# Scatters in pairs behind named matmul groups, and fills behind the second score pass

## The chip, the cores and the metric

The kernel runs on one core of one Trainium2 chip. The metric is the time of one execution on the device, in microseconds, as the median of several runs. Engines are named as the profile names them: PE (TensorE), DVE (VectorE), ACT (ScalarE), POOL (GpSimd) and SP (SyncE).

## The reference

For `x` of 16 x 512 tokens with 256 features in float32:

```
xn  = layernorm(x)
att = softmax(causal(rope(xn Wq) rope(xn Wk)^T / 4)) (xn Wv) Wo      # 16 heads of 16
s   = softmax(xn router_w^T + router_bias);  top 4 of 32 experts, their scores rescaled to a sum of 1
moe = sum over the 4 of score * down_e(silu(gate_e xn) * up_e xn)    # hidden size 128
sh  = (silu(xn sgate^T) * (xn sup^T)) sdown^T                        # shared, hidden size 512
out = x + att + moe + sh
```

## The kernel before, in words

`block_kernel` runs three phases. Phase A (`phase_a`) goes over the 16 batches of 512 tokens and computes layernorm, attention, the shared network and the routing. It also writes each token's normalised row, once for each of its four experts, into that expert's region of the DRAM tensor `values`, and a small entry (where the result goes, and its weight) into `table`. Phase B/C (`phase_bc`) is the expert loop: 288 blocks of 128 rows are loaded from `values`, go through their expert, and are scattered to `y_dram`. Phase D adds the four results of each token and the rest, and stores `out`.

**Order of the work in phase A.** All engines walk one list of steps, `ORDER`, from line 74. Each engine has a table of handlers (`run`, and the dictionaries that are given to it) and carries out, in the list's order, the steps that it has a handler for. Nothing reorders an engine's own queue: an instruction that waits for a semaphore holds up all behind it on that engine. Steps named in `NEXT_STEPS` (layernorm, xT, qk, vr, part0, part1, partsT, stack, route and the ranks) work on the next batch, so the list overlaps batch b's attention with batch b+1's projections. The first and second batch's steps are written out, batches 1 to 14 are a hardware loop, and the last batch (`last_steps`) leaves the next-batch steps out.

**The steps that matter here.**
- `s1 g u` (PE, L949 and L952) makes the scores of heads of group g in their first form; DVE (L745) takes their row maxima. `negsplit` (DVE) splits the negative maxima into three bf16 parts, `negT` transposes them (PE L962, ACT L595), and SP (L403) copies them by DMA into extra rows of `q_st`. `s2 g u` (PE L982 and L993) then makes the transposed scores with the maxima already subtracted; it waits for that DMA at u = 0. ACT (L607) takes the exponential of each s2 group.
- s1 and s2 write to two PSUM units in turn (`ps_u`), so a group waits for the reader of the group but one before it: DVE's maximum for an s1, ACT's exponential for an s2.
- `qk t` for tile t of the next batch: PE projects (L911), DVE applies the rotary factors (L706, L709) into two buffers, POOL adds them into `rqk` (L472), ACT copies that to bf16 in step `part0` (L542), POOL subtracts (L474), ACT copies the rest in step `part1` (L547), POOL subtracts again (L476). PE transposes the three parts in `partsT` (L923). All of POOL's part is one handler, at the step `qk t`; ACT's parts stand at their own places in the list, among exponentials.
- `copy` (ACT L585) copies the normalised rows to `xs` once all scatters of the batch before have landed (`scattered`); DVE's `rankC` waits for the same and makes `slot`.
- `scat t` (POOL L487, L489) issues, for the four choices of tile t, one indirect DMA to `table` and one to `values`: 8 for a step, 32 for a batch. Steps scat 0 and 1 stand early in the list, after `gth 1` and `gth 2`; scat 2 and 3 stand after `partsT 3` and `s2 3 0`, behind qk 3.
- `fill` (POOL L495), in the last batch alone, behind scat 3: 32 indirect DMAs of zero rows, one for each expert, so that the last block of each region is complete. Phase A ends when `filled` and `scattered` have their full counts and SP's last store has landed.

What the scatter step and its neighbours on POOL's queue look like before:

```
def scatter(b, step, env):
    t = step[1]
    pool.wait_ge(xs_ready, NT * b + NT)
    pool.wait_ge(slots, b + 1)
    hold(pool, passed_pool)
    for k in range(TOPK * t, TOPK * (t + 1)):
        ...
run(pool, {"loaded": loaded, "qk": qkv, "scat": scatter, "fill": fill})
```

Of the kernel before, what the change touches and what calls it, by code (L numbers as in the profile page):

```python
# [34 lines left out]
BATCH, SEQ, D = 16, 512, 256  # L35
NT = SEQ // P
KC = D // P
NH, DH = 16, 16
NG, GH = 4, 4
E, TOPK, HE, HS = 32, 4, 128, 512  # L40
NM = HS // P
# [19 lines left out]
NU1 = len(MAX_UNITS)  # L61
NU2 = GH + 1


def hold(eng, passed):


    eng.sem_inc(passed, 1)
# [4 lines left out]

ORDER = [
    ("rankC",), ("gate", 0), ("placeV",), ("s1", 0, 0), ("gth", 0), ("up", 0), ("s1", 0, 1), ("copy",), ("s1", 0, 2),
    ("gate", 1), ("s1", 0, 3), ("s1", 0, 4), ("gth", 1), ("scat", 0), ("up", 1), ("lnA",), ("gate", 2), ("s1", 0, 5),
    ("negsplit", 0), ("gth", 2), ("scat", 1), ("s1", 1, 0), ("up", 2), ("s1", 1, 1), ("negT", 0), ("gate", 3),
# [11 lines left out]
    ("exps",), ("stack", 1), ("down", 0), ("down", 1), ("rankA",), ("av", 3, 0), ("av", 3, 1), ("av", 3, 2),  # L89
    ("av", 3, 3), ("rankB",), ("down", 2), ("avT", 3), ("down", 3), ("aT", 0), ("aT", 1), ("oproj", 0), ("oproj", 1),  # L90
]


def attention_steps(with_next):
# [3 lines left out]
def last_steps(order):  # L98


    s, piece = [], 0
    for step in order:
        s.append(step)
        if step == ("rankC",):
            s.append(("fill_rows",))
        if step == ("scat", NT - 1):
            s.append(("fill",))
        if step[0] == "s2" and step[1:] != (0, 0) and piece < GU_PIECES:
            s.append(("load_gu", piece))
            piece += 1  # L110
        if step == ("s2", NG - 1, NU2 - 1):
            s += [("load_d", k) for k in range(D_PIECES)]
    assert piece == GU_PIECES
    return s
# [75 lines left out]
def phase_a(nc, sb_, sem, ident, identb, iota_e, counts, we_gu, we_d, ps_g, ps_u, ps_av, x, wqkvr, wgu_e, wd_e, wo, wgu_s, wd_s, bias,  # L190
            rope_cos, rope_sin, values, sum_dram, table):
    stack = ExitStack()
    with stack:
        def sb(name, shape, dt=F32):
            return sb_(name, shape, dt, stack)

        def carve(space):
# [3 lines left out]
            def take(shape, dt=F32):  # L201
# [6 lines left out]
                if len(names) == 1:  # L208
# [54 lines left out]
        av = sb("av", [P, SEQ])  # L263
# [5 lines left out]
        gth = sb("gth", [P, SEQ])  # L269
# [18 lines left out]
        slot = sb("slot", [P, NT * TOPK], I32)  # L288
        dest_f = sb("dest_f", [P, NT * TOPK])
        entry = sb("entry", [P, NT * TOPK, 2], I32)  # L290
        xs = sb("xs", [P, NT, D])
# [4 lines left out]
        xs_ready, slots = sem("xs_ready"), sem("slots")  # L296
# [3 lines left out]
        scattered = sem("scattered")  # L300
# [4 lines left out]
        we_in, fill_chain, fill_ready, filled = sem("we_in"), sem("fill_chain"), sem("fill_ready"), sem("filled")  # L305
        neg_parts, tanh_done, av_out, exps, chosen_ready = \
            sem("neg_parts"), sem("tanh_done"), sem("av_out"), sem("exps"), sem("chosen_ready")
        pe = {n: sem("pe_" + n) for n in ("xT", "qk", "vr", "qT", "kT", "gate", "up", "s1", "negT", "s2", "av", "avT",
                                          "aT", "sum", "rank")}
# [11 lines left out]
        block = stack.enter_context(nc.Block())  # L321
        body = attention_steps(True)
        tail = last_steps(attention_steps(False))


# [96 lines left out]
        def _(pool):  # L422
# [56 lines left out]
                    chain.closed()  # L479

            def scatter(b, step, env):
                t = step[1]
                pool.wait_ge(xs_ready, NT * b + NT)
                pool.wait_ge(slots, b + 1)
                hold(pool, passed_pool)
                for k in range(TOPK * t, TOPK * (t + 1)):
                    pool.indirect_dma_start(table[:, :], bass.IndirectOffsetOnAxis(ap=slot[:, k:k + 1], axis=0),  # L487
                                            entry[:, k, :], None).then_inc(scattered, 16)
                    pool.indirect_dma_start(values[:, :], bass.IndirectOffsetOnAxis(ap=slot[:, k:k + 1], axis=0),  # L489
                                            xs[:, k // TOPK, :], None).then_inc(scattered, 16)  # L490

            def fill(b, step, env):
                pool.wait_ge(fill_ready, 1)
                for e in range(E):
                    pool.indirect_dma_start(values[:, :], bass.IndirectOffsetOnAxis(ap=fill_row[:, e:e + 1], axis=0),  # L495
                                            zeros[:, :], None, bounds_check=E * REGION - 1, oob_is_err=False
                                            ).then_inc(filled, 16)

            def loaded(b, step, env):
                if step[1] == 1:  # L500
# [6 lines left out]
                    pool.wait_ge(table_set, 16)  # L507

            run(pool, {"loaded": loaded, "qk": qkv, "scat": scatter, "fill": fill})
            pool.wait_ge(filled, 16 * E)  # L510
            pool.wait_ge(scattered, SCATTERS * BATCH)
# [983 lines left out]
```

## Time and profile before

| | before |
|---|---|
| median of 3 runs | 2137.58 us (2136.33 to 2138.6) |
| profiled execution, its span | 2641.3 us (no other time is given for this execution) |
| PE busy | 1935.0 us, 73% |
| POOL busy | 1063.8 us, 40% |
| DVE busy | 1290.2 us, 49% |
| ACT busy | 929.5 us, 35% |
| mean granted clock of PE | 0.847 |

The runs are executions without the profiler; the profiled one is longer by 503.7 us. Phase A takes the first 1945 us of the profiled span, the expert loop the stretch to about 2525, phase D the rest. A row of a timeline gives the start in us from the span's start, the busy time in us, engine, line and operation, and in brackets how long the engine was idle before it and what ended that wait.

### The profile page before, as it was taken

What the parts mean: (1) busy time and instruction counts of PE and PEld (TensorE: products, weight loads), DVE (VectorE), ACT (ScalarE), POOL (GpSimd) and SP (SyncE); (2) the same over time, 40 slices, a digit from 0 to 9 for tenths busy, and PEclk for the clock granted to TensorE, in tenths of its full rate; (3) what the DMA queues carried; (4) which work ended last, traced back from release to release, by engine and by line L of the source; (5) the groups of instructions that cost most, each with busy time, mean ns of one, the idle gap of its engine ahead of it and who ended that gap; (6) DMA issues with size and microseconds to landing.
All of it is one profiled execution on the core that took longest, in us unless ns stands there. A gap on an engine that the chain in (4) does not pass through costs nothing. (4 is left out here: it accounts for less than half of the span.)

```text
span 2641.3 us, 43971 instructions
## 1 busy us (share of the span) xinstructions
PE 1935.0 (73%) x11495; PEld 1234.2 (47%) x11496; DVE 1290.2 (49%) x3379; ACT 929.5 (35%) x1953; POOL 1063.8 (40%) x1056
## 2 busy tenths in 40 slices
PE   5677778787767878777887877874479898998900
PEld 2344444444434444444544444442257777777700
DVE  4445345364534536453453535442235555555567
ACT  2324252443415244242534424341224444444400
POOL 5444343343434334443433444246215544554500
PEclk8888788898878888887988888887689999999955
DMA  5150423415052341505225051432455554545389
GB/s 107 63 97 21 93 40 64 64 40 96 19 94 40 64 64 40 96 22 90 47 57 88 17 100 30 78 59 76 132 158 159 153 150 146 155 144 152 112 304 331
DMA packets 242512, 255.07 MB, mean 97 GB/s; under 512 B 74357, under 2 KB 216190, under 8 KB 242304
## 3 DMA queue, kind: packets, MB, share of 16 engines
q1 hardware_dynamic: 184768, 161.63, 28.4%
q0 software_dynamic: 35840, 71.63, 8.6%
q10 hardware_dynamic: 21824, 20.98, 2.5%
q14 instruction: 60, 0.49, 0.1%
q8 instruction: 20, 0.33, 0.1%
HBM read 112.54 MB, written 94.64 MB: 78 GB/s over the span
## 5 line engine op out<-in xcount | busy, mean ns | idle before, releaser
L745 DVE TENSOR_REDUCE neg<-ps_u 128x2 f32<-128x768 f32 (+3 forms) x384 | 392.4, 1043 | 380.7 <-PE ps_u L952 237.2
L487 POOL DMA_INDIRECT table<-entry,slot x256 | 248.0, 969 | 536.2 <-ACT xs L585 435.4
L982 PE MATMUL ps_u<-we_d 99*128 99x512 bf16 (+3 forms) x1024 | 246.1, 353 | 250.1 <-DMA we_d<-neg_t 121.6
L607 ACT ACTIVATE probs<-ps_u 128x1024 f32<-128x1024 f32 x320 | 323.1, 1027 | 286.6 <-PE ps_u L993 189.2
L1244 POOL DMA_INDIRECT y_dram<-yb,ent x288 | 283.0, 983 | 278.8 <-issue 164.9
L489 POOL DMA_INDIRECT values<-xs,slot x256 | 252.3, 986 | 83.4 <-issue 83.4
L933 PE MATMUL ps_g<-we_gu 128*128 128x512 f32 x512 | 257.7, 634 | 38.1 <-DVE hid L728 32.1
L949 PE MATMUL ps_u<-we_d 96*128 96x128 bf16 (+3 forms) x1024 | 232.2, 312 | 72.4 <-ACT probs L607 26.6
L982 PEld LDWEIGHTS ps_u<-we_d 99*128 99x128 bf16 x1024 | 96.5, 107 | 397.5 <-issue 221.4
L911 PE MATMUL ps_g<-we_gu 128*128 128x512 f32 (+1 forms) x512 | 199.7, 514 | 2.4 <-ACT we_gu L564 2.4
L472 POOL TENSOR_TENSOR rqk<-we_gu 128x512 f32<-128x512 f32 x64 | 81.3, 1270 | 266.2 <-DVE we_gu L709 263.3
L767 DVE RECIPROCAL rden<-ps_g 128x16 f32<-128x16 f32 x64 | 16.3, 255 | 348.8 <-issue 250.2
L1281 PE MATMUL ps_av<-we_gu,x_t 128*128 x576 | 157.9, 399 | 36.5 <-DVE x_t L1369 34.5
L1012 PE MATMUL ps_av<-probs,v_pad 128*32 128x512 f32 (+3 forms) x2048 | 165.9, 447 | 23.8 <-issue 22.6
L949 PEld LDWEIGHTS ps_u<-we_d 96*128 96x128 bf16 x1024 | 94.1, 100 | 190.5 <-issue 59.8
L1295 PE MATMUL ps_u<-we_d,h_t 128*128 x576 | 177.6, 391 | 0.0
L952 PE MATMUL ps_u<-mask_qk,identb 128*128 128x128 bf16 (+2 forms) x704 | 177.2, 252 | 0.0
L993 PE MATMUL ps_u<-mask_kq,identb 128*128 128x256 bf16 (+1 forms) x640 | 132.6, 291 | 52.1 <-issue 52.1
L933 PEld LDWEIGHTS ps_g<-we_gu 128*128 128x128 f32 x512 | 97.2, 200 | 132.1 <-issue 80.5
L1281 PE MATMUL ps_g<-we_gu,x_t 128*128 x576 | 155.4, 394 | 4.1 <-issue 4.1
L1369 DVE COPY x_t<-ps_g 128x256 f32<-128x256 f32 x288 | 120.6, 419 | 67.9 <-issue 44.8
L616 ACT ACTIVATE av<-ps_av 128x512 f32<-128x512 f32 x64 | 37.8, 591 | 299.6 <-remote 212.1
(158 smaller groups left out, 3247.4 us busy)
## 6 DMA issues: line engine op xcount, KB each, us to landing
we_d<-we_gu SPq DMA_DIRECT2D x384, 128.0 KB, 5.9
xg<-values SPq DMA_DIRECT2D x288, 128.0 KB
ys<-y_dram SPq DMA_DIRECT2D x64, 512.0 KB, 5.4
we_gu<-x SPq DMA_DIRECT2D x16, 512.0 KB
xres<-x SPq DMA_DIRECT2D x16, 512.0 KB
sum_dram<-osum SPq DMA_DIRECT2D x16, 512.0 KB, 3.2
we_gu<-wgu_e ACTq DMA_DIRECT2D x16, 512.0 KB
sums_in<-sum_dram SPq DMA_DIRECT2D x8, 1024.0 KB
```

The lines of the kernel that those rows point to most:

```text
L487: pool.indirect_dma_start(table[:, :], bass.IndirectOffsetOnAxis(ap=slot[:, k:k + 1], axis=0), entry[:, k, :], None).then_inc(scattered, 16)
L489: pool.indirect_dma_start(values[:, :], bass.IndirectOffsetOnAxis(ap=slot[:, k:k + 1], axis=0), xs[:, k // TOPK, :], None).then_inc(scatte ...
L607: nc.scalar.activation(probs[g % 2][:, u, :], ps_u[env[1][step][0]][:, :, :].rearrange("p a n -> p (a n)"), ACT.Exp, scale=SCALE).then_inc ...
L745: nc.vector.tensor_reduce(neg[:, g % 2, i, h0:h0 + nh], src, AX.X, ALU.max, negate=True).then_inc(S["row_max"], 1)
L911: ins = nc.tensor.matmul(ps[:, 0:n], xn_t[:, c, t * P:(t + 1) * P], w_qkvr[:, c, lo:lo + n], start=(c == 0), stop=(c == KC - 1))
L933: ins = nc.tensor.matmul(ps[:, :], w_gu[:, c, lo:lo + P], xn_t[:, c, :], start=(c == 0), stop=(c == KC - 1))
L949: nc.tensor.matmul(ps[:, a, k * n:(k + 1) * n], q_st[0:KROWS, h, i * P:(i + 1) * P], k_st[0:KROWS, h, 0:n], start=(k == 0), stop=False, sk ...
L952: ins = nc.tensor.matmul(dst, identb[:], mask_qk[:].rearrange("p (o n) -> p o n", o=1).broadcast_to([P, per_bank, P]), start=False, stop=T ...
L982: nc.tensor.matmul(ps[:, a, lo:lo + n], k_st[0:MROWS, h, kt * P:(kt + 1) * P], q_st[0:MROWS, h, kt * P:SEQ], start=(lo == 0), stop=False, ...
L1244: pool.indirect_dma_start(y_dram[:, :], bass.IndirectOffsetOnAxis(ap=ent[k][:, 0:1], axis=0), yb[k][:, :], None, bounds_check=TOKENS * TOP ...
L1281: ins = nc.tensor.matmul(ps_gu[s][:, 0:2 * HE], x_t[s][:, c * P:(c + 1) * P], w_gu[:, bass.ds(e, 1), c, :], start=(c == 0), stop=(c == KC ...
L1295: nc.tensor.matmul(ps_y[s][:, 0:D], h_t[s][:], w_d[:, bass.ds(e, 1), :], start=True, stop=True).then_inc(y_ps, 1)
```

## The change

`scat` becomes 16 steps instead of 4. Step k issues one pair: the DMA to `table` and the DMA to `values` of column k of `slot`. Each waits first for a matmul group that `SCAT_AFTER[k]` names, by PE's semaphore for it; only k = 0 waits for `xs_ready` and `slots`. In `ORDER` the 16 steps are spread over the list, each behind its group. Nothing else in the list changes place. The 32 fills of the last batch become 16 steps of two, each behind an s2 group that `FILL_AFTER` names. The number of DMAs is the same.

```
--- before.py
+++ after.py
 ORDER = [
     ("rankC",), ("gate", 0), ("placeV",), ("s1", 0, 0), ("gth", 0), ("up", 0), ("s1", 0, 1), ("copy",), ("s1", 0, 2),
-    ("gate", 1), ("s1", 0, 3), ("s1", 0, 4), ("gth", 1), ("scat", 0), ("up", 1), ("lnA",), ("gate", 2), ("s1", 0, 5),
...
+    ("gate", 1), ("s1", 0, 3), ("scat", 0), ("s1", 0, 4), ("gth", 1), ("up", 1), ("scat", 1), ("lnA",), ("gate", 2),
+    ("s1", 0, 5), ("scat", 2), ("negsplit", 0), ("gth", 2), ("s1", 1, 0), ("up", 2), ("scat", 3), ("s1", 1, 1),
+    ("negT", 0), ("gate", 3), ("lnB",), ("lnC",), ("gth", 3), ("up", 3), ("scat", 4), ("s2", 0, 0), ("s2", 0, 1),
+    ("s2", 0, 2), ("s1", 1, 2), ("scat", 5), ("xT", 0), ("xT", 1), ("xT", 2), ("s1", 1, 3), ("s1", 1, 4), ("qk", 0),
+    ("s2", 0, 3), ("vr", 0), ("xT", 3), ("vr", 1), ("part0", 0), ("s1", 1, 5), ("negsplit", 1), ("s2", 0, 4),
+    ("scat", 6), ("qk", 1), ("part1", 0), ("negT", 1), ("s1", 2, 0), ("s1", 2, 1), ("part0", 1), ("av", 0, 0),
+    ("av", 0, 1), ("s1", 2, 2), ("s2", 1, 0), ("scat", 7), ("av", 0, 2), ("av", 0, 3), ("s1", 2, 3), ("partsT", 0),
+    ("s1", 2, 4), ("s1", 2, 5), ("scat", 8), ("part1", 1), ("avT", 0), ("qk", 2), ("s2", 1, 1), ("s2", 1, 2),
+    ("negsplit", 2), ("partsT", 1), ("s2", 1, 3), ("scat", 9), ("part0", 2), ("qk", 3), ("s2", 1, 4), ("negT", 2),
+    ("part1", 2), ("vr", 2), ("s1", 3, 0), ("s1", 3, 1), ("scat", 10), ("part0", 3), ("av", 1, 0), ("av", 1, 1),
...
+    ("av", 2, 2), ("av", 2, 3), ("s2", 3, 0), ("scat", 14), ("s2", 3, 1), ("avT", 2), ("stack", 0), ("s2", 3, 2),
+    ("s2", 3, 3), ("scat", 15), ("rank",), ("s2", 3, 4),
...
+SCAT_AFTER = [("s1", 0, 3), ("up", 1), ("s1", 0, 5), ("up", 2), ("up", 3), ("s1", 1, 2), ("s2", 0, 4), ("s2", 1, 0),
+              ("s1", 2, 5), ("s2", 1, 3), ("s1", 3, 1), ("s2", 2, 0), ("s2", 2, 3), ("s2", 2, 4), ("s2", 3, 0),
+              ("s2", 3, 3)]
+
+
+FILL_AFTER = [(0, 3), (0, 4), (1, 0), (1, 1), (1, 2), (1, 3), (1, 4), (2, 0), (2, 1), (2, 2), (2, 3), (2, 4), (3, 0),
+              (3, 1), (3, 2), (3, 3)]
+FILLS = 2
...
-        if step == ("scat", NT - 1):
-            s.append(("fill",))
+        if step[0] == "s2" and step[1:] in FILL_AFTER:
+            s.append(("fill", FILL_AFTER.index(step[1:])))
...
             def scatter(b, step, env):
-                t = step[1]
-                pool.wait_ge(xs_ready, NT * b + NT)
-                pool.wait_ge(slots, b + 1)
+                k = step[1]
+                after = SCAT_AFTER[k]
+                if after[0] == "s1":
+                    pool.wait_ge(pe["s1"], NG * NU1 * b + NU1 * after[1] + after[2] + 1)
+                elif after[0] == "s2":
+                    pool.wait_ge(pe["s2"], NG * NU2 * b + NU2 * after[1] + after[2] + 1)
+                else:
+                    pool.wait_ge(pe["up"], NM * b + after[1] + 1)
+                if k == 0:
+                    pool.wait_ge(xs_ready, NT * b + NT)
+                    pool.wait_ge(slots, b + 1)
                 hold(pool, passed_pool)
-                for k in range(TOPK * t, TOPK * (t + 1)):
...
+                pool.indirect_dma_start(table[:, :], bass.IndirectOffsetOnAxis(ap=slot[:, k:k + 1], axis=0),
+                                        entry[:, k, :], None).then_inc(scattered, 16)
+                pool.indirect_dma_start(values[:, :], bass.IndirectOffsetOnAxis(ap=slot[:, k:k + 1], axis=0),
+                                        xs[:, k // TOPK, :], None).then_inc(scattered, 16)
 
             def fill(b, step, env):
-                pool.wait_ge(fill_ready, 1)
-                for e in range(E):
+                k = step[1]
+                if k == 0:
+                    pool.wait_ge(fill_ready, 1)
+                pool.wait_ge(pe["s2"], NG * NU2 * (BATCH - 1) + NU2 * FILL_AFTER[k][0] + FILL_AFTER[k][1] + 1)
+                for e in range(FILLS * k, FILLS * (k + 1)):
```

## Rows read from the trace of the kernel before

**Rows 1.** The page: its span, and one of its costliest groups.

```profile
span 2641.3 us, 43971 instructions
...
L1244 POOL DMA_INDIRECT y_dram<-yb,ent x288 | 283.0, 983 | 278.8 <-issue 164.9
```

**Rows 2.** Windows of one batch: start:end, length, each engine's busy time, clock, DMA share, GB/s.

```profile
994.00:1004.00 10.00, 9.97 (x42) 4.68 (x41) 9.41 (x20) 1.19 (x2) 7.05 (x8) 1.00 0.31 104
...
1020.50:1024.00 3.50, 3.48 (x15) 1.75 (x15) 1.61 (x4) 1.94 (x2) 0.00 (x0) 0.50 0.00 0
...
1044.00:1054.00 10.00, 10.00 (x90) 5.89 (x89) 6.43 (x12) 7.03 (x11) 4.71 (x5) 1.00 0.00 1
...
1070.00:1083.40 13.40, 2.57 (x7) 0.62 (x6) 0.00 (x0) 0.00 (x0) 7.74 (x8) 0.50 0.99 163
1083.40:1089.00 5.60, 5.53 (x31) 3.60 (x31) 0.68 (x2) 4.47 (x5) 0.00 (x0) 0.50 0.00 0
...
sum 115.70, PE 88.80 PEld 50.88 DVE 56.02 ACT 42.72 POOL 45.64; mean PE 6.34 PEld 3.63 DVE 4.00 ACT 3.05 POOL 3.26
```

**Rows 3.** Timeline of POOL, one batch: start, us, line, op, idle before and releaser.

```profile
1030.30 1.27 POOL L472 TENSOR_TENSOR rqk<-we_gu 128x512 f32<-128x512 f32 x1 [15.43 <-DVE we_gu L709]
...
1035.90 1.27 POOL L472 TENSOR_TENSOR rqk<-we_gu 128x512 f32<-128x512 f32 x1 [0.24 <-DVE we_gu L709]
...
1042.92 1.15 POOL L476 TENSOR_TENSOR we_gu<-we_gu 128x512 bf16<-128x512 f32 x1 [3.85 <-ACT we_gu L547]
1045.88 1.27 POOL L472 TENSOR_TENSOR rqk<-we_gu 128x512 f32<-128x512 f32 x1 [1.80 <-DVE we_gu L709]
...
1052.96 1.27 POOL L472 TENSOR_TENSOR rqk<-we_gu 128x512 f32<-128x512 f32 x1 [0.17 <-POOL we_gu L476]
...
1058.36 1.16 POOL L476 TENSOR_TENSOR we_gu<-we_gu 128x512 bf16<-128x512 f32 x1 [2.23 <-ACT we_gu L547]
1059.67 0.99 POOL L487 DMA_INDIRECT table<-entry,slot  x1 [0.15 <-issue]
1060.96 0.97 POOL L489 DMA_INDIRECT values<-xs,slot  x1 [0.31 <-issue]
...
1109.74 0.97 POOL L487 DMA_INDIRECT table<-entry,slot  x1 [29.68 <-ACT xs L585]
...
1225.43 0.97 POOL L487 DMA_INDIRECT table<-entry,slot  x1 [29.93 <-ACT xs L585]
```

**Rows 4.** Timeline of ACT in the same batch.

```profile
1037.21 0.63 ACT L542 ACTIVATE we_gu<-rqk 128x512 bf16<-128x512 f32 x1 [1.70 <-POOL rqk L472]
...
1048.92 0.66 ACT L542 ACTIVATE we_gu<-rqk 128x512 bf16<-128x512 f32 x1
...
1054.27 0.63 ACT L542 ACTIVATE we_gu<-rqk 128x512 bf16<-128x512 f32 x1 [2.42 <-POOL rqk L472]
```

**Rows 5.** Timeline of PE in the same batch.

```profile
1040.74 0.38 PE L949 MATMUL ps_u<-we_d 96*128 96x512 bf16 x1
...
1050.82 0.38 PE L949 MATMUL ps_u<-we_d 96*128 96x256 bf16 x2
...
1056.35 0.39 PE L949 MATMUL ps_u<-we_d 96*128 96x512 bf16 x1
...
1086.41 1.06 PE L982 MATMUL ps_u<-we_d 99*128 99x512 bf16 x3
```

**Rows 6.** Window from the last batch's first scatter to its last matmul.

```profile
1792.00:1941.00 149.00, 71.27 (x441) 38.51 (x439) 34.69 (x57) 27.36 (x33) 62.51 (x64) 0.71 0.39 129
```

**Rows 7.** Timelines of POOL, SP and PE, last batch: its ends, the negative-row transfer.

```profile
1792.57 0.97 POOL L487 DMA_INDIRECT table<-entry,slot  x1 [29.38 <-ACT xs L585]
...
1873.30 0.98 POOL L495 DMA_INDIRECT values<-zeros,fill_row  x1 [0.30 <-issue]
...
1813.80 104.16 SPq L403 DMA_DIRECT2D we_d<-neg_t  x4
...
1816.14 1.01 PE L982 MATMUL ps_u<-we_d 99*128 99x512 bf16 x3 [9.41 <-DMA we_d<-neg_t]
```

More of the change, by code:

```diff
@@ L75 @@
     ("rankC",), ("gate", 0), ("placeV",), ("s1", 0, 0), ("gth", 0), ("up", 0), ("s1", 0, 1), ("copy",), ("s1", 0, 2),
-    ("gate", 1), ("s1", 0, 3), ("s1", 0, 4), ("gth", 1), ("scat", 0), ("up", 1), ("lnA",), ("gate", 2), ("s1", 0, 5),
-    ("negsplit", 0), ("gth", 2), ("scat", 1), ("s1", 1, 0), ("up", 2), ("s1", 1, 1), ("negT", 0), ("gate", 3),
[11 rows of a table removed]
+    ("gate", 1), ("s1", 0, 3), ("scat", 0), ("s1", 0, 4), ("gth", 1), ("up", 1), ("scat", 1), ("lnA",), ("gate", 2),
+    ("s1", 0, 5), ("scat", 2), ("negsplit", 0), ("gth", 2), ("s1", 1, 0), ("up", 2), ("scat", 3), ("s1", 1, 1),
+    ("negT", 0), ("gate", 3), ("lnB",), ("lnC",), ("gth", 3), ("up", 3), ("scat", 4), ("s2", 0, 0), ("s2", 0, 1),
[9 rows of a table added]
+    ("negsplit", 3), ("route",), ("partsT", 3), ("s2", 2, 4), ("scat", 13), ("negT", 3), ("av", 2, 0), ("av", 2, 1),
+    ("av", 2, 2), ("av", 2, 3), ("s2", 3, 0), ("scat", 14), ("s2", 3, 1), ("avT", 2), ("stack", 0), ("s2", 3, 2),
+    ("s2", 3, 3), ("scat", 15), ("rank",), ("s2", 3, 4),
     ("exps",), ("stack", 1), ("down", 0), ("down", 1), ("rankA",), ("av", 3, 0), ("av", 3, 1), ("av", 3, 2),
@@ L481, in scatter @@
             def scatter(b, step, env):
-                t = step[1]
-                pool.wait_ge(xs_ready, NT * b + NT)
-                pool.wait_ge(slots, b + 1)
-                hold(pool, passed_pool)
-                for k in range(TOPK * t, TOPK * (t + 1)):
[L487 to L490, printed above, removed]
-            def fill(b, step, env):
-                pool.wait_ge(fill_ready, 1)
-                for e in range(E):
+                k = step[1]
[9 more added lines that the diff above has]
+                    pool.wait_ge(slots, b + 1)
+                hold(pool, passed_pool)
+                pool.indirect_dma_start(table[:, :], bass.IndirectOffsetOnAxis(ap=slot[:, k:k + 1], axis=0),
+                                        entry[:, k, :], None).then_inc(scattered, 16)
+                pool.indirect_dma_start(values[:, :], bass.IndirectOffsetOnAxis(ap=slot[:, k:k + 1], axis=0),
+                                        xs[:, k // TOPK, :], None).then_inc(scattered, 16)
+            def fill(b, step, env):
+                k = step[1]
[3 more added lines that the diff above has]
+                for e in range(FILLS * k, FILLS * (k + 1)):
                     pool.indirect_dma_start(values[:, :], bass.IndirectOffsetOnAxis(ap=fill_row[:, e:e + 1], axis=0),
```

13 rows, old and new, of the table ORDER are left out of this document.

## The prediction

> **What bounds the kernel now.** The page comes first [rows 1]: the profiled span is 2641.3 us and the median of the runs 2137.58 us, 503.7 us less. So part of what the trace shows cannot be in the runs, and the first question is which part. The windows of one batch [rows 2] show it: while POOL issues long bursts of scatters, all other engines stand nearly still (from 1070.0 to 1083.4 PE is busy 2.57 of 13.4 us, DVE and ACT not at all), and after such a stretch TensorE's granted clock is 0.50, the 1.2 GHz level, for a few us. Between bursts (1044 to 1054) PE is busy 10.0 of 10 us at clock 1.00: there the order of PE's work is the bound.
>
> **Budget.** A batch lasts 115.7 us (1109.74 to 1225.43 [rows 3]), PE is busy 88.80 of it [rows 2], idle 26.9. There are 15 such batches: 403.5 us. The last batch has 149.0 − 71.3 = 77.7 us of idle [rows 6]. The two windows at clock 0.50 (3.5 and 5.6 us) would take half at the full clock: 4.55 a batch, some 73 us in all. Together 554 us could vanish, and 504 have. What is left, 50 us or 3.1 us a batch, is about what plain waits between PE, ACT and DVE need. I read it so: the standstills belong to the profiled execution, and in the runs a batch takes about 86 us with PE nearly always busy. The other bound: the expert loop's scatters (L1244 [rows 1]) are idle 278.8 us, 164.9 of it their own pace; if the other 114 us were missing from the runs as well, (50 + 114) / 16 = 10.3 us of idle a batch would still be real, 7 above the plain waits.
>
> **The change, part by part.**
>
> *Removed: bursts of 16 scatters.* Each batch issues the same 32 scatters, so POOL's total is the same. What a burst could cost in the runs is a late transfer of the negative row maxima, which s2 waits for. In the last batch that transfer is issued at 1813.80, amid 64 indirect DMAs without a gap from 1792.57 on, and s2 starts at 1816.14 [rows 7]: 2.3 us. That is short, so I take a gain of 0; the bounds are 0 and 7 us a batch (above).
>
> *Moved: four pairs into the middle of the rope chain.* On POOL's queue pair 6 now stands ahead of qk 1, pairs 7 and 8 ahead of qk 2, pair 9 ahead of qk 3. Before, nothing stood there. Two scatters are 1.29 us apart start to start and the first begins 0.15 us after a tensor operation ends (1059.67, 1060.96 [rows 3]), so a pair takes 2.6 us and two take 5.1. All four matmul groups that they name are done by the time POOL arrives, so the gates wait for nothing. I follow the chain POOL, ACT, PE, since part0 stands on ACT's queue ahead of an exponential, and that exponential frees the PSUM unit that PE's next group but one needs:
> - qk 0 ends at 1035.66 (0.24 before 1035.90 [rows 3]); pair 6 runs to 1038.3; rqk 1 starts at 1038.5, not 1035.90: +2.6. part0 of tile 1 moves from 1037.21 [rows 4] to 1039.8, the exponential of s2(1,0) behind it ends at 1041.4, and s1(2,4) starts at 1041.5, not 1040.74 [rows 5]: PE +0.8. The last subtraction of qk 1 waited 3.85 us for ACT [rows 3], so it loses only 1.0: it ends at 1045.1, not 1044.07.
> - pairs 7 and 8 run to 1050.2; rqk 2 starts at 1050.4, not 1045.88 [rows 3]: +4.5. part0 of tile 2 goes from 1048.92 [rows 4] to 1051.7, s2(1,4)'s exponential ends at 1053.3, s1(3,1) starts at 1053.4, not 1050.82 [rows 5]: PE +2.6 by now. qk 2 ends at 1055.7, not 1052.79: +2.9.
> - pair 9 runs to 1058.3; rqk 3 starts at 1058.5, not 1052.96: +5.5. part0 of tile 3 already waited for it (2.42 us [rows 4]), so it moves from 1054.27 to 1059.8, s2(2,0)'s exponential ends at 1061.8, and s1(3,4) starts at 1061.9, not 1056.35 [rows 5]: PE +5.6 by now.
>
> With a little for the register arithmetic of four gates: 5.7 us a batch. PE has no idle time afterwards in which to win it back (88.8 us busy [rows 2], 84 of it at the full clock, in a batch of 86 to 91). The 15 batches that work on a next one pay it: 85.5 us. Bounds: 2.6 a batch if ACT and PE absorb the last step, 7.5 if each pair costs 3.0 us and a wait more.
>
> *Moved: the other pairs.* Pairs 0 to 5 take 15.6 us between the copy and rope 0, where POOL waited 15.43 us beside its burst (1030.30 [rows 3]), some 4 without the standstill; pair 5, gated by s1(1,2), is over before that rope. Pairs 10 to 15 go out behind qk 3, the last behind s2(3,3) (from 1086.41 [rows 5] to 1087.3), over by 1090, with the copy just before 1109.74. Cost 0, hidden by POOL's wait before the copy (29.68 us [rows 3], some 13 of it left without the standstills); were it gone, each further us would be on ACT's copy.
>
> *The last batch.* It has no rope work. Before, POOL issued 64 indirect DMAs solidly from 1792.57 to 1874.3 [rows 7]. PE ended at 1941.0, but less 77.7 of idle, with some 5 for the clock and 5 of plain waits given back to either side, at about 1864: in the runs POOL ends this phase, by some 8 us. After, POOL is idle in part until s2(0,3), about 1812.5 without the wait of 9.41 us [rows 7]; from there 26 pairs (16 of fills, 10 of scatters) at 2.58 keep it busy for 67 us, to 1879.6: +5. Bounds 0 and 10.
>
> Sum: 85.5 + 5 = 90.5 us more; on the median of the runs, 2228 us. Against the profiled execution itself the sum would be 2732, but the profile of the changed kernel will not show that: spread pairs should not bring the standstills, so its span should fall, to some 2300 to 2500 us, while the runs get longer.
>
> **A rule that would make it worse.** In the window 994 to 1004, DVE is busy 9.41 of 10 us and POOL's scatters keep their 0.97 us, as they do at 1070 to 1083.4 with DVE idle (7.74 us for 8) [rows 2]: DVE doesn't hold them up. The Trainium skill, SBUF — State Buffer, section on the two separate sides, says that GpSimd cannot write descriptors for its DMAs while a VectorE operation in a two-port mode holds their shared port. The windows with both busy speak against it for these operations. By that rule the time would be nearer to the 2348 us of the last but one rival.
>
> **The rivals.**
> - *Faster.* The standstills are partly real, at the start of s2(0,0) and of s2(3,0), up to 7 us a batch, and single pairs end them: 16 × 7 = 112 less. With half of the chain's cost (2.6 × 15 + 5 = 44) the time is 2070; with a gain of 6 a batch, 2086. It decides from the point where the real stall exceeds what the pairs cost the rope chain. For it: the 163 GB/s and DMA share 0.99 at 1070 [rows 2]. Against: the budget, and the 2.3 us of the transfer. Taken as 2085. Chance 0.13.
> - *A smaller loss.* The chain delays PE only up to s1(3,1), +2.6 a batch, or the gain takes half of it: 39 + 5, 2182. Chance 0.15.
> - *No change.* POOL frees itself for the next tensor operation as soon as a DMA is handed on, so a pair costs nothing, or gain and loss cancel: 2138. Chance 0.04. Against: 0.97 us busy for each.
> - *DVE holds up the pairs in the rope chain* by one reduce of about 1 us for each of 8 scatters: 8 more a batch, 2137.6 + 15 × 13.7 + 5 = 2348. Chance 0.02.
> - *The gates do nothing*, each being open already when POOL comes to it: for pairs 6 to 9 this is so and is part of the forecast; for all 16 it would leave the same cost in the rope chain.
>
> **How the numbers follow.** The forecast, 2228, has 0.66 and a range of its own from 2195 to 2258: the cost of a batch from 4 to 7.5, with 0 to 10 for the end. With the smaller loss, from 2150 up, this holds about 0.8. 0.2% (4 us) is about what a measurement of this kernel can tell. Slower by more: 0.66 + 0.15 + 0.02 = 0.83; within it 0.04; faster 0.13.
>
> **What would show it.** In the profile after: POOL's rqk of tiles 1 to 3 start right after a scatter and not on DVE; ACT's part0 waits for POOL by several us each; PE waits for ACT's exponential at s1(3,1) and s1(3,4); the idle of 29.7 us before the copy shrinks; 64 indirect DMAs end the phase. It is wrong if these waits are there and the time is not above 2142 (then the standstills were real in part), or if rqk 2 and 3 start no later, against their ropes, than before.

## The result and the profile after

The changed kernel takes 2208.51 us (median of 4 runs, 2199.36 to 2209.38); the kernel before, beside it, 2136.95 us. The ratio is 1.033, with a 95% interval of 1.0309 to 1.035: 71.6 us slower. Forecast were 90.5 us more (2228 us, range 2150 to 2258).

One plain fact has to be known before the traces are compared. The kernel before does not take the same time on every chip: in the series below it took 2137 us on one chip and 2639 to 2642 us on three others, and in all series the profiled execution was as long as the runs beside it. The trace of before that stands above has a span of 2641.3 us and a mean granted clock of 0.847, where the runs of before in the series have 0.94 on the one chip and 0.85 on the three, so I take it to be of the second sort; the runs of before that stand beside it are of the first, and so are the runs and the trace (span 2197.5) of the changed kernel that are shown here. I call them chips without and with standstills, for short: each chip was used in one series alone, so that it is the chip, and not something that changed from series to series, is not shown. Rows of the two traces can be compared in the stretches without a standstill only.

The page of the changed kernel, span, busy time and the costliest group on POOL (to be held against [rows 1]):

```profile
span 2197.5 us, 44375 instructions
...
PE 1819.5 (83%) x11495; PEld 1188.7 (54%) x11496; DVE 1276.1 (58%) x3379; ACT 923.8 (42%) x1953; POOL 1064.8 (48%) x1056
...
L506 POOL DMA_INDIRECT table<-entry,slot x256 | 249.7, 975 | 441.3 <-PE ps_u L974 322.1
```

One batch of it in a window (the sum row of [rows 2] is the one before). A batch lasts 89.0 us here (791.62 to 880.64 on POOL) and 89.9 in the mean of 14, from POOL's rqk of tile 0 to the next batch's. PE is busy 80.75 us of the window and the clock is 0.98 of the full one, so no standstill is in it:

```profile
880.00:969.00 89.00, 80.75 (x550) 48.10 (x548) 53.09 (x126) 42.12 (x67) 45.84 (x44) 0.98 0.39 69
```

POOL in that batch, start and busy time first, idle time and releaser in brackets ([rows 3] before). The rqk of tile 0 starts at 900.48, before at 1030.30; so 129.82 us are added to compare. Tile 1 then starts at 1038.11 (before 1035.90, +2.2), tile 2 at 1049.65 (1045.88, +3.8), tile 3 at 1057.23 (1052.96, +4.3), each with no idle time behind a scatter. From tile 0 to tile 3 it is 26.93 us in the median of 15 batches, and 22.66 before. The rows:

```profile
900.48 1.26 POOL L484 TENSOR_TENSOR rqk<-we_gu 128x512 f32<-128x512 f32 x1 [2.12 <-DVE we_gu L731]
...
908.29 1.28 POOL L484 TENSOR_TENSOR rqk<-we_gu 128x512 f32<-128x512 f32 x1
...
913.69 1.15 POOL L488 TENSOR_TENSOR we_gu<-we_gu 128x512 bf16<-128x512 f32 x1 [2.23 <-ACT we_gu L569]
...
919.83 1.28 POOL L484 TENSOR_TENSOR rqk<-we_gu 128x512 f32<-128x512 f32 x1
...
927.41 1.27 POOL L484 TENSOR_TENSOR rqk<-we_gu 128x512 f32<-128x512 f32 x1
...
934.12 0.98 POOL L506 DMA_INDIRECT table<-entry,slot  x1
...
948.87 0.97 POOL L508 DMA_INDIRECT values<-xs,slot  x1 [0.30 <-issue]
```

ACT's part0 of tiles 1 to 3 ([rows 4] before) waits for POOL, 4.70 us at the last, where it was 2.42:

```profile
909.60 0.63 ACT L564 ACTIVATE we_gu<-rqk 128x512 bf16<-128x512 f32 x1 [3.90 <-POOL rqk L484]
...
921.13 0.63 ACT L564 ACTIVATE we_gu<-rqk 128x512 bf16<-128x512 f32 x1 [1.60 <-POOL rqk L484]
...
928.72 0.63 ACT L564 ACTIVATE we_gu<-rqk 128x512 bf16<-128x512 f32 x1 [4.70 <-POOL rqk L484]
```

PE at the three places of the forecast, and the next batch's last wait for the negative rows ([rows 5] before). Shifted by 129.82, s1(2,4) is 0.3 us late, s1(3,1) 1.7 and s1(3,4) 4.3, and the two longer waits are put down to ACT's exponential:

```profile
911.19 0.39 PE L971 MATMUL ps_u<-we_d 96*128 96x512 bf16 x1
...
922.73 0.39 PE L971 MATMUL ps_u<-we_d 96*128 96x256 bf16 x2 [1.30 <-ACT probs L629]
...
930.80 0.39 PE L971 MATMUL ps_u<-we_d 96*128 96x512 bf16 x1 [2.67 <-ACT probs L629]
...
943.21 0.59 PE L1004 MATMUL ps_u<-we_d 99*128 99x512 bf16 x3 [0.83 <-DMA we_d<-neg_t]
```

The end of the last batch ([rows 7] before): POOL, then PE's last group, then two windows. POOL issues its last DMA at 1505.67, 5 us after PE is done, and the next phase begins 9.55 us after that one is over. The DMA engines are idle for most of this wait, with a share of 0.08 up to 1511 and 0.00 behind it:

```profile
1505.67 0.97 POOL L508 DMA_INDIRECT values<-xs,slot  x1 [0.30 <-issue]
1516.19 0.37 POOL L1254 IOTA blk_i<- 32x288 f32 x1 [9.55 <-POOLq L205]
```

```profile
1496.81 3.72 PE L1073 MATMUL ps_u<-w_o,attn_t 128*128 128x256 f32 x16 [0.25 <-ACT attn_t L644]
```

```profile
1506.00:1511.00 5.00, 0.00 (x0) 0.00 (x0) 0.00 (x0) 0.00 (x0) 0.64 (x1) 0.50 0.08 26
1511.00:1516.00 5.00, 0.00 (x0) 0.00 (x0) 0.00 (x0) 0.00 (x0) 0.00 (x0) 0.50 0.00 0
```

Over the whole run PE waits 64.7 us for the exponential ahead of an s1 group; with the four pairs out of the chain (e1, below) it is 2.3 us:

```profile
PE ps_u L971 <- ACT probs L629: 64.7, 34, 5.3
```

```profile
PE ps_u L971 <- ACT probs L629: 2.3, 7, 0.7
```

The difference, 62.4 us, is as much as this execution (2199.36 us, the fastest of the four) takes beyond the 2136.95 of before. The other three take 2208 to 2209 us, with a mean granted clock of 0.931 to 0.933 where this one has 0.939 and the runs of before on the first series' chip 0.940 to 0.944. So the 9 us between them are not in this trace, and a lower clock goes with them.

### The profile page after: what moved, and what is told of

Its sections match the earlier page's. It is cut to its first block and busy times, and to the rows that moved or that the text cites. A ratio compares the mean times of both kernels' runs of the same rounds, so it can differ in the third digit from the quotient of the medians.

```text
span 2197.5 us, 44375 instructions
## 1 busy us (share of the span) xinstructions
PE 1819.5 (83%) x11495; PEld 1188.7 (54%) x11496; DVE 1276.1 (58%) x3379; ACT 923.8 (42%) x1953; POOL 1064.8 (48%) x1056
## 5 line engine op out<-in xcount | busy, mean ns | idle before, releaser
L629 ACT ACTIVATE probs<-ps_u 128x1024 f32<-128x1024 f32 x320 | 317.8, 1023 | 140.2 <-PE ps_u L1015 138.8
L971 PE MATMUL ps_u<-we_d 96*128 96x128 bf16 (+3 forms) x1024 | 225.2, 304 | 95.3 <-ACT probs L629 64.7
L955 PE MATMUL ps_g<-we_gu 128*128 128x512 f32 x512 | 242.8, 607 | 3.0 <-DVE gth L742 2.9
L1004 PE MATMUL ps_u<-we_d 99*128 99x512 bf16 (+3 forms) x1024 | 199.0, 307 | 29.1 <-ACT probs L629 9.0
L1004 PEld LDWEIGHTS ps_u<-we_d 99*128 99x128 bf16 x1024 | 88.7, 99 | 129.4 <-issue 57.2
L1034 PE MATMUL ps_av<-probs,v_pad 128*32 128x512 f32 (+3 forms) x2048 | 156.0, 440 | 0.6 <-ACT probs L629 0.6
L1398 DVE TENSOR_SCALAR wh<-ent 128x1 f32<-128x1 f32 x288 | 44.3, 154 | 173.4 <-ACT tnh L1213 137.1
L599 ACT ACTIVATE we_gu<-ps_g 128x512 f32<-128x512 f32 x64 | 38.2, 597 | 219.1 <-PE ps_g L955 219.1
L1303 PEld LDWEIGHTS ps_av<-we_gu,x_t 128*128 128x128 f32 x576 | 102.0, 198 | 43.1 <-issue 34.8
L1227 ACT ACTIVATE yb<-ps_u 128x256 f32<-128x256 f32 x288 | 110.3, 383 | 34.1 <-PE ps_u L1317 8.3
```

Source lines behind the costliest of these rows:

```text
L629: nc.scalar.activation(probs[g % 2][:, u, :], ps_u[env[1][step][0]][:, :, :].rearrange("p a n -> p (a n)"), ACT.Exp, scale=SCALE).then_inc ...
L955: ins = nc.tensor.matmul(ps[:, :], w_gu[:, c, lo:lo + P], xn_t[:, c, :], start=(c == 0), stop=(c == KC - 1))
L971: nc.tensor.matmul(ps[:, a, k * n:(k + 1) * n], q_st[0:KROWS, h, i * P:(i + 1) * P], k_st[0:KROWS, h, 0:n], start=(k == 0), stop=False, sk ...
L1004: nc.tensor.matmul(ps[:, a, lo:lo + n], k_st[0:MROWS, h, kt * P:(kt + 1) * P], q_st[0:MROWS, h, kt * P:SEQ], start=(lo == 0), stop=False, ...
L1303: ins = nc.tensor.matmul(ps_gu[s][:, 0:2 * HE], x_t[s][:, c * P:(c + 1) * P], w_gu[:, bass.ds(e, 1), c, :], start=(c == 0), stop=(c == KC ...
```

## The experiments

Twelve runs in four series. The first (e1, e6, e7, e8) ran on a chip without standstills (before 2136.69 us, 9 runs), the second (e2, e3, e4, e5), third (e9, e10, e11) and fourth (e12) on three chips with them (2639.25, 2641.85 and 2640.54 us). Times are compared within a series.

### First series: which pairs cost what

**e1_chain_free.** Pairs 6 to 9 go behind qk 3, all else as changed.

```
-    ... ("s2", 0, 4), ("scat", 6), ("qk", 1), ... ("s2", 1, 0), ("scat", 7), ... ("s1", 2, 5), ("scat", 8), ...
-    ... ("s2", 1, 3), ("scat", 9), ("part0", 2), ("qk", 3), ...
+    ... ("s2", 1, 3), ("part0", 2), ("qk", 3), ("scat", 6), ("scat", 7), ("scat", 8), ("scat", 9), ...
```

> The changed kernel with pairs 6 to 9 moved behind qk 3 on POOL's queue, gates and fills unchanged. Theory A (the loss is POOL's pairs in the rope chain, some 4.3 us a batch by the trace after, and the rest is the end of the last batch): 2144 us, 2138 to 2150, 65 below the changed kernel. Theory B (the gates, or the spreading itself, cost time wherever the pairs stand): it stays near 2208. Theory C (bursts also hold PE up in the runs, and single pairs gain that back): with the chain free the gain shows, below 2130.

Measured: 2227.9 us (2222.28 to 2233.4), ratio 1.042 [1.0392, 1.0447]. All three theories missed. POOL and DVE show why; POOL first, rqk of tile 3 and the last scatter of the batch, then DVE's `rankC`, then PE:

```profile
844.87 1.27 POOL L484 TENSOR_TENSOR rqk<-we_gu 128x512 f32<-128x512 f32 x1 [0.17 <-POOL we_gu L488]
...
876.09 0.97 POOL L508 DMA_INDIRECT values<-xs,slot  x1 [0.30 <-issue]
```

```profile
885.02 0.18 DVE L860 TENSOR_TENSOR entry<-pr,zs 128x16 f32<-128x16 f32 x1 [5.48 <-DMA values<-xs,slot]
```

```profile
888.13 0.50 PE L971 MATMUL ps_u<-we_d 96*128 96x384 bf16 x1 [4.78 <-DVE neg L767]
```

The chain is free: rqk of tile 3 follows tile 2 after 0.17 us, as before. But ten pairs now stand behind qk 3; the last is issued at 876.09, over at 877.06, and `rankC`, which waits for `scattered`, starts at 885.02: the last scatter lands 8 us after POOL is done with it. DVE stands idle 5.48 us, and PE 4.78 us behind it. Over the whole run this wait is 74.5 us in 15 batches; PE's wait for DVE's maxima ahead of an s1 group grows by 65.5 us (14.0 in the changed kernel, 79.5 here), and its wait for the exponential falls by 62.4 (64.7 to 2.3). So the loss of the chain was given back at another place, and the cover that I had counted on for the pairs behind qk 3 is thin.

That alone does not make the kernel slower than the changed one. PE is also busy for longer, 1841.2 us against 1819.5, with the same instructions: behind the wait of 4.78 us its granted clock is 0.50, the 1.2 GHz level, for some 5 us of its work (888 to 893).

```profile
888.00:890.00 2.00, 1.87 (x6) 1.02 (x7) 1.87 (x4) 0.00 (x0) 0.00 (x0) 0.50 0.00 0
890.00:892.00 2.00, 2.00 (x4) 0.74 (x3) 1.48 (x2) 0.00 (x0) 0.00 (x0) 0.50 0.00 0
```

The three together, −62.4 + 65.5 + 21.7, give 24.8 us more than the changed kernel; the two profiled executions differ by 30.9.

The same run settles what a burst does on such a chip. Windows of the stretch with scatters and SP's stack copies (cf. 1070 to 1083.4 in [rows 2]: DMA share 0.99, 163 GB/s, PE busy 2.57 of 13.4):

```profile
861.00:871.00 10.00, 9.72 (x78) 6.57 (x79) 2.32 (x10) 4.64 (x7) 7.56 (x8) 1.00 1.14 169
871.00:881.00 10.00, 9.75 (x50) 7.65 (x49) 2.07 (x4) 1.52 (x3) 4.84 (x5) 1.00 1.12 180
```

DMA share and GB/s are higher than there, the row of scatters is longer (20), and PE is busy 9.72 and 9.75 of 10 us.

**e6_pair9_only** and **e7_pair6_only.** Of the four pairs one stays in the chain, the others go behind qk 3.

```
e6:  ... ("s2", 1, 3), ("scat", 9), ("part0", 2), ("qk", 3), ("scat", 6), ("scat", 7), ("scat", 8), ...
e7:  ... ("s2", 0, 4), ("scat", 6), ("qk", 1), ... ("qk", 3), ("scat", 7), ("scat", 8), ("scat", 9), ...
```

> Pair 9 alone stays ahead of qk 3; 6, 7 and 8 go behind it. Theory A: rqk of tile 3 followed qk 2 at once before the change and ACT waited for it, so one pair there costs its full 2.2 us a batch: 15 x 2.2 = 33 above the kernel with a free chain, 2177 us. If the loss were shared evenly by the four pairs it would be 16, 2160. Theory B: near 2208.

> Pair 6 alone stays ahead of qk 1; 7, 8 and 9 go behind qk 3. Theory A: the chain has slack there (POOL's last subtraction of tile 1 waited 3.85 us for ACT before), PE loses 0.3 us a batch: 2144 + 4 = 2148. Shared evenly: 2160. Theory B: near 2208.

Measured: 2216.64 us (2215.53 to 2221.15) and 2193.39 us (2187.94 to 2195.68). Both are some 40 us above the expectation of theory A, and the wait of `rankC` that e1 showed is nearly as long. The waits, in us in total, times, longest, first e6, then e7:

```profile
DVE entry L860 <- DMA values<-xs,slot: 40.3, 15, 5.0
...
PE ps_u L971 <- ACT probs L629: 37.7, 19, 2.4
```

```profile
DVE entry L860 <- DMA values<-xs,slot: 43.2, 15, 5.1
...
PE ps_u L971 <- ACT probs L629: 2.3, 7, 0.7
```

With nine pairs behind qk 3 the wait of `rankC` is 40.3 and 43.2 us, 2.7 to 2.9 a batch, against 5.0 with ten and none with six. Taking it off leaves 2176.3 and 2150.2 us, where 2177 and 2148 were expected for the chain. So close an agreement is in part luck: the same taken off e1 leaves 2153.4, 9 above the 2144 expected, and PE itself waits for DVE only 32.8 and 35.2 us longer than in the changed kernel (46.8 and 49.2 against 14.0), which would leave 2183.8 and 2158.2. The difference of the two kernels, 23.3 us or 1.6 a batch, does not depend on it: pair 9 costs more than pair 6, and they do not share evenly. PE's wait for the exponential says the same, 37.7 us with pair 9 alone and 2.3 with pair 6 alone, as in e1.

**e8_six_pairs.** Pairs 10 and 11 too stand ahead of qk 3, with gates that are open.

```
-    ... ("s2", 1, 3), ("scat", 9), ("part0", 2), ("qk", 3), ...
+    ... ("s2", 1, 3), ("scat", 9), ("part0", 2), ("scat", 10), ("scat", 11), ("qk", 3), ...
```

> Pairs 10 and 11 too stand ahead of qk 3, six pairs in the chain in place of four (their gates name s2(1,3)). Theory A: no slack is left there, so the two cost their full 2 x 2.5 us a batch: 15 x 5.1 = 77 above the changed kernel, 2285 us. Theory B: no difference, 2208.

Measured: 2296.95 us (2294.46 to 2299.17), 88 above the changed kernel, 77 expected. PE's wait for the exponential ahead of an s1 group, in the changed kernel and here:

```profile
PE ps_u L971 <- ACT probs L629: 64.7, 34, 5.3
```

```profile
PE ps_u L971 <- ACT probs L629: 140.3, 34, 10.4
```

It grows by 75.6 us, 5.0 a batch, which is what two pairs take on POOL (2 x 2.55). The chain has no slack left, as expected. The profile shows where the other 12 us can lie: PE is busy 1843.0 us, 23.5 longer than in the changed kernel with the same instructions, at a mean granted clock of 0.911 against 0.939.

### Second and third series: gates, fills, bursts

**e2_no_gates.** The handler without its waits for matmul groups; the order on POOL's queue is the same.

```
 def scatter(b, step, env):
     k = step[1]
-    after = SCAT_AFTER[k]
-    if after[0] == "s1":
-        pool.wait_ge(pe["s1"], ...)
...
     if k == 0:
```

> The changed kernel without the waits for matmul groups; the order on POOL's queue is the same. Pairs 0 to 5 then go out in one stretch behind the copy and 10 to 15 behind qk 3. Theory A: the four pairs in the rope chain stay where they are and their gates were open anyway, so the batches keep their loss and only the last batch starts earlier: 2204, 2198 to 2210. Theory B (the waits themselves cost): falls by 20 or more, under 2190. If the gates had saved something by thinning the DMAs, it rises above 2212.

Measured: 2517.95 us (2512.79 to 2522.68), before 2639.25, ratio 0.954. The numbers expected were for the other sort of chip, and whether closed gates cost or save anything there is not tested. Twelve scatters in a row behind the copy, and twelve behind qk 3, go with waits of PE that are longer than the changed kernel's on such a chip (4.28 and 3.08 us at the same places, e11 below); the first is at the end of the batch before, the longest of its kind, the second at s2(0,0):

```profile
802.43 4.49 PE L1027 MATMUL ps_av<-probs,v_pad 128*32 128x512 f32 x32 [11.30 <-ACT probs L622]
...
854.02 1.04 PE L997 MATMUL ps_u<-we_d 99*128 99x512 bf16 x3 [6.56 <-ACT probs L622]
```

**e3_fills_paired.** The kernel before, with the fills alone in gated pairs; the fill handler and `FILL_AFTER` as in the change.

```
-        if step == ("scat", NT - 1):
-            s.append(("fill",))
+        if step[0] == "s2" and step[1:] in FILL_AFTER:
+            s.append(("fill", FILL_AFTER.index(step[1:])))
```

> The kernel before, with the fills alone in 16 pairs behind the second score pass. Theory A: POOL is busy without a gap from the copy on in either order, so the last batch ends at the same time: 2137, 2133 to 2141. Rival: the gated fills themselves make the end later, 2142 to 2150. All other batches have their bursts: if the standstills belong to the profiled execution, the profile here shows a span several hundred us above its runs.

Measured: 2606.48 us (2604.58 to 2607.36), ratio 0.9875 [0.9858, 0.9892]; span of the profiled execution 2603.9. The last sentence of the expectation is refuted: the execution is as long as its runs. So the standstills are in all runs on these chips. The pairing of the fills saves 33 us here; what it does on a chip without standstills this run cannot tell.

**e5_last_as_before** and **e10_last_as_before_2.** The changed kernel; in the last batch all scatters and fills stand ungated in one row behind `gth 1`.

```
     for step in order:
+        if step[0] == "scat":
+            continue
         s.append(step)
+        if step == ("gth", 1):
+            s += [("scat", k) for k in range(16)] + [("fill", 0)]
...
-FILLS = 2
+FILLS = E
```

> The changed kernel, with the last batch's 32 scatters and 32 fills ungated in one row behind the copy, as before. Theory A: POOL ends the last batch, and it loses some 5 us to gates at its start; without them 2202, 4 to 8 below the changed kernel. Rival: PE or the weight loads end that phase, 2208.

> The changed kernel with the last batch's scatters and fills ungated in one row, a second time. On a chip where before takes 2137: 2202, some 6 below the changed kernel (POOL ends that phase and starts earlier). Rival there: 2208, the landing of the last DMAs and not POOL's start sets the end. On a chip where before takes 2639 it is above the changed kernel, at 2420 as the first time, since the long row brings the standstill back.

Measured: 2420.03 us (2417.99 to 2435.72) on one chip, 2428.25 us (2425.64 to 2433.36) on the other. Beside the changed kernel on the second chip (2396.98, below) one unbroken row of 64 costs 31 us; in the two traces the batches before it are equally long (100.4 and 100.5 us) and the last stretch is 40 us longer (table below). The question that it was made for, what the gated last batch costs without standstills, stays open.

**e4_fills_burst.** The changed kernel with its 32 fills behind pair 15 in one row.

```
-        if step[0] == "s2" and step[1:] in FILL_AFTER:
-            s.append(("fill", FILL_AFTER.index(step[1:])))
+        if step == ("scat", 15):
+            s.append(("fill", 0))
...
-FILLS = 2
+FILLS = E
```

> The changed kernel with its 32 fills in one burst behind pair 15. Theory A: POOL idles between gated pairs in the last batch and then has 41 us of fills from s2(3,3) on, some 20 us past its present end: 2228, 2222 to 2235. Rival (POOL does not end the phase): 2208.

Measured: 2387.15 us (2386.31 to 2392.73), ratio 0.9051. e5 was 8 us lower on this chip than the same kernel (e10) on the other; with as much for the chip, the changed kernel would be at about 2389 here. By that the burst at the end costs nothing against pairs, while by the two traces the last stretch is 5.3 us longer with it (193.5 and 188.2). That is a comparison over two chips and decides nothing; the numbers expected were for a chip without standstills and are not tested.

**e11_changed_again.** The changed kernel, nothing edited, on a chip with standstills.

> The changed kernel as it is. The kernel before took 2137 us on one chip and 2639 on another, with the same instructions, so the standstills are real on some chips. On a chip where before takes 2137: 2208. On a chip where before takes 2639: theory D (a long unbroken row of indirect DMAs brings the standstill there, single pairs with pauses bring little of it): 2370, 2340 to 2400, a ratio of 0.90 and below all variants tried there. Theory E (the number of DMAs counts and not their spacing): 2639 + 72 = 2710.

Measured: 2396.98 us (2386.37 to 2400.51), before 2641.85, ratio 0.9085 [0.9066, 0.9105]; span of the profiled execution:

```profile
span 2384.5 us, 44375 instructions
```

The same change that costs 3.3% on one chip saves 9.1% on another. Theory D holds in direction and size, E falls. Not all of D came true: e4, on another such chip, was lower still (ratio 0.9051). Nor do the pairs end the standstills: a batch takes 100.5 us here and 89.9 on the chip without them. PE's two long waits of one batch, in the same places as the standstills of before, are 4.28 and 3.08 us:

```profile
840.52 4.46 PE L1034 MATMUL ps_av<-probs,v_pad 128*32 128x512 f32 x32 [4.28 <-ACT probs L629]
...
887.25 0.61 PE L1004 MATMUL ps_u<-we_d 99*128 99x512 bf16 x3 [3.08 <-DMA we_d<-neg_t]
```

**e9_balanced** and **e12_balanced_again.** An attempt at both: 7 pairs ahead of qk 0, one ahead of qk 1 (in the slack), 8 behind qk 3 as before, and the last batch of e5.

```
+    ... ("s1", 1, 2), ("scat", 5), ("scat", 6), ... ("s2", 0, 4), ("scat", 7), ("qk", 1), ...
+    ... ("part0", 2), ("qk", 3), ("scat", 8), ("scat", 9), ... ("s1", 3, 1), ("scat", 10), ...
```

> Pairs 0 to 6 ahead of qk 0, pair 7 ahead of qk 1, pairs 8 to 15 behind qk 3, the last batch as before: the rope chain keeps one pair, in its slack, and rankC no longer waits for late landings, since only 8 pairs stand behind qk 3 as before. Theory A with the second wait (rankC behind the landing of the last scatters) that the first series showed: on a chip where before takes 2137 it gives 2141, 2135 to 2150. If gates or single pairs cost anything by themselves: above 2160. On a chip where before takes 2639: near 2450, since 8 pairs behind qk 3 are again an unbroken row.

> Pairs 0 to 6 ahead of qk 0, pair 7 ahead of qk 1, pairs 8 to 15 behind qk 3, last batch as before, a second time. On a chip where before takes 2137: both waits of the first series (the rope chain; rankC behind the landing of the last scatters) should be gone, 2141, 2135 to 2150; if gates or single pairs cost anything by themselves, above 2160. On a chip where before takes 2639: 2436 as the first time.

Measured: 2436.04 us (2431.69 to 2440.64) and 2432.96 us (2429.75 to 2441.79), ratios 0.9233 and 0.922. Both series fell on chips with standstills, so the half of the expectation that mattered is untested. On them e12 came out as expected, and e9 at 2436 where near 2450 was expected. Both are slower than the changed kernel, but the order of the pairs is not what makes them so. e10 has the changed kernel's order in the batches and the same last batch, and on e9's chip it takes 2428.25 us: the balanced order costs 8 us, the ungated last batch the other 31. The traces say the same. A batch is the mean of 14, from POOL's rqk of tile 0 to the next batch's; the last stretch goes from the last such row to POOL's first operation of the next phase (L1254 in the changed kernel); both in us:

| run | sort of chip | batch | last stretch |
|---|---|---|---|
| the changed kernel | without | 89.9 | 164.6 |
| the changed kernel, e11 | with | 100.5 | 188.2 |
| e10 | with | 100.4 | 228.2 |
| e9, e12 | with | 101.1, 101.0 | 226.5, 228.7 |
| e2 | with | 109.0 | 200.2 |
| before | with | 114.8 | 231.7 |
| e3 | with | 114.5 | 202.5 |

The rows for the last stretch of e9, and then of e10:

```profile
1511.85 1.28 POOL L486 TENSOR_TENSOR rqk<-we_gu 128x512 f32<-128x512 f32 x1
...
1738.39 0.37 POOL L1257 IOTA blk_i<- 32x288 f32 x1 [71.33 <-POOLq L207]
```

```profile
1499.71 1.27 POOL L486 TENSOR_TENSOR rqk<-we_gu 128x512 f32<-128x512 f32 x1 [2.58 <-DVE we_gu L734]
...
1727.91 0.37 POOL L1257 IOTA blk_i<- 32x288 f32 x1 [73.47 <-POOLq L207]
```

In the batches, tile 3's rqk starts 22.95 us behind tile 0's, against 26.93 in e11, so the chain gives back 4.0 us, and yet the batch is 0.6 longer: an estimate from the two is that standstills take 4.6 us more. The standstills behind qk 3 are in the trace, here of e12: PE's matmuls come a few at a time with 1.4 to 2.7 us between them and nothing that the profile shows to wait for:

```profile
847.03 1.24 PE L1007 MATMUL ps_u<-we_d 99*128 99x512 bf16 x3 [2.70 <-issue]
850.12 0.26 PE L1018 MATMUL ps_u<-mask_kq,identb 128*128 128x128 bf16 x1 [1.85 <-issue]
851.77 0.37 PE L1018 MATMUL ps_u<-mask_kq,identb 128*128 128x256 bf16 x1 [1.39 <-issue]
```

## Why the prediction was right, and where not

**The sign and the main term.** The forecast was that four pairs in the rope chain hold up POOL, then ACT, then PE. The rows of after show each link, and e8 shows the slope: two pairs more, 5.0 us a batch more. PE's wait for the exponential follows the pairs in the chain: 2.3 us with none (e1) or pair 6 alone (e7), 37.7 with pair 9 alone (e6), 64.7 with the four, 140.3 with six (e8). Taken from the trace the cost is 4.3 us a batch, 15 x 4.3 = 64 us of the 71.6. The term was mis-sized: 5.7 predicted, 4.3 measured. I let each pair take 2.6 us with an idle 0.3 behind its last DMA, but a tensor operation follows a DMA at once (908.29, no idle), so a pair takes 2.2 to 2.3 at its place and tile 3 is 4.3 late, not 5.5. At s1(2,4) PE lost 0.3 and not 0.8: pair 6 holds up rqk 1 by 2.2 and not 2.6, and the exponential starts 0.1 us before part0 is over. That all gates would be open, that the first part has slack, and that the last pair costs its full length because ACT already waited there: as predicted, and e7 and e6 tell the two apart (23.3 us between them). The forecast's own range does not quite follow from its bounds: 60 and 122.5 us more are 2198 and 2260, not 2195 and 2258. One limit: there is no trace of before on a chip without standstills, so the 4.3 us compare a quiet stretch of a trace from one chip with a trace from another. What the forecast of the loss left out is the clock: behind PE's wait of 4.78 us in e1 the granted clock is 0.50, behind its 2.67 us at 930.80 in the changed kernel it is 0.53 (933 to 936), and PE's busy time is 22 us longer in e1 and 23.5 in e8. For the change itself this cannot be separated from the rest.

**The last batch.** Predicted +5. The rest of the result, 71.6 − 64 = 7.6 us, is of that size, but that does not confirm the term: the profiled execution is only 62.4 us longer than before and so leaves nothing for it, and no run isolates it on that sort of chip. What the trace does show: the first scatter starts at 1421.85, 4.1 us behind the copy and not 0.8 as before, since it waits for its gate, s1(0,3); the 64 DMAs then take 84.8 us where they took 81.7, and 66.9 of it from the first fill on, where 67 were predicted. That POOL ends this phase is right for the changed kernel: its last DMA goes out 5 us after PE's last group. For before it was worked out and not seen. The 9.55 us from the end of this DMA to the next phase were left out of the forecast; they are 9.5 to 9.6 us in all five traces of such a chip, and what they consist of is not shown.

**The other pairs, cost 0.** True of the change itself (`rankC` does not wait there), but the cover was named wrongly. I named ACT's copy as the one that waits, with some 13 us to spare. In e1 the first to wait is `rankC` on DVE, and landing takes 8 us from the end of the issue; one pair more behind qk 3 than the eight of before pays 2.7 to 2.9 us (e6, e7).

**The reading of the standstills.** This step of the prediction failed, though the time came out in the range. I argued from 504 us between span and runs, and a budget that fitted, that the standstills belong to the profiled execution. They do not: in the second and third series every run has them (2639 and 2642 us for before, 2606 for e3 with a span of 2603.9). They go with the chip, or the series, that a kernel runs in. The budget's number was right for the runs that I had to forecast (about 86 us a batch: 89.9 less 4.3 is 85.6), since these came from a chip without them; that it was so is luck and not the argument's doing, and e1 shows that a longer row of scatters, with more DMA traffic, leaves PE at 9.7 of 10 us there. But "a gain of 0" fits such chips only; on the others the gain is larger than the loss, 245 us net. The forecast that the profile of after would show 2300 to 2500 us, longer than its runs, came true in neither trace: the one above has 2197.5, and e11 has 2384.5 but is as long as its runs.

**The rivals.** "Faster, since single pairs end the standstills" decides on chips with standstills, with 0.9085 and not the 0.975 that I gave it: the mechanism was right there in that single pairs shorten the standstills (they do not end them), and its price was far too small. "Smaller loss" (+2.6 a batch) and "no change" are excluded by 4.3, and by 64.7 us of wait. DVE holding up the pairs is excluded: all scatters of the rope chain take 0.96 to 0.99 us. "The gates do nothing" holds for the four in the chain; for the others it is open, since the only run without gates (e2) fell on a chip with standstills.

## What to carry to other kernels

Work that is put on an in-order queue between the links of a chain cost its full length here where the next link already waited, and almost nothing where the chain had slack: read it link by link. A wait of some us can cost more than its length, as in e1, where the clock was lower behind it: compare PE's busy time as well as its waits. Work that is moved behind the chain to spare it must still land, so look at who waits for the landing and not for the issue. And when a profiled execution and the runs differ by a fifth, compare the profile with runs beside that very execution, before anything is called an artefact. Compare a variant with the run that shares all but one of its edits, too: e9 looked like a failure of its order until e10 stood beside it. The chip can decide the sign: the same edit was 3% slower on one chip and 9% faster on another.

## What was not expected of the hardware

- The kernel before takes 2137 us on one chip and 2640 us on three others, repeatably within a series (9, 9, 7 and 11 runs, each set within 1%). The difference lies mostly in stretches with long unbroken rows of indirect DMAs, in which PE, DVE and ACT nearly stop and POOL keeps its pace of 1.27 us. A part of 8 to 15 us lies behind phase A: that stretch takes 681.3 us in the trace of the changed kernel without standstills and 689.4 to 696.2 in those with them. What stalls is not shown: much of the idle time there has no releaser in the profile ("issue").
- Spacing matters there and not the count alone: with the same DMAs a batch takes 114.8 us with two rows of 16, 109.0 with rows of 12 (no gates), 101 with 16 behind qk 3 of which the first 12 are unbroken, 100.5 with gated pairs; the last batch's stretch is 227 to 232 us with one row of 64 and 188.2 with gated pairs.
- An indirect DMA from POOL can be followed by a tensor operation with no idle time, while two indirect DMAs have 0.30 us between them.
- The last scatter of a batch lands 8 us after POOL is done with it while other DMAs run beside it (e1, DMA share above 1 from 876 to 886). The 9.55 us at the end of phase A are no such case: the DMA engines are idle for most of them.
- Behind a wait of 4.78 us PE's granted clock is 0.50 for some 5 us (e1), so that wait cost more than its own length.

Open: what the gated last batch and the closed gates cost on a chip without standstills, whether the balanced order is as fast as before there, and what brings the standstills.
